# A graph layer's node loop: h and z transposed through memory in quarters instead of on TensorE, and 23 scatters moved into the pair stage

## The chip, the cores and the metric

The kernel runs on one core of one Trainium2 chip, in one launch. The metric is the device time in microseconds; several runs give a median. Besides there is one execution under the hardware profiler. Its engines are PE (TensorE), DVE (VectorE), ACT (ScalarE), POOL (GpSimd) and SP (SyncE, which only issues transfers here).

## The reference

A layer of a graph attention network with a feed-forward part, on 50,000 nodes of 256 features and 12,500 edges, in fp32. Every node also has an edge to itself.

```python
h = jnp.maximum(_layernorm(x, axis=-1), 0.0)
# _L0_gnn_ref(h): attention over edges (8 heads of 32), then
out = jax.ops.segment_sum(msg, dst, num_segments=n)
out = out.reshape(n, H * C) + bias
h = _layernorm(out + x, ln1_g, ln1_b)                # here x is the h from above
ff = jax.nn.gelu(h @ ffn_W1.T + ffn_b1, approximate=False) @ ffn_W2.T + ffn_b2
return _layernorm(h + ff, ln2_g, ln2_b)
# and at the end: x = x + _L0_gnn_ref(...)
```

Only some 12,000 nodes at most have an edge besides the one to themselves. The kernel therefore computes messages and a correction record for the destinations of the 12,500 edges, and a node loop computes for all 50,000 nodes h @ W_src (the node's edge to itself), adds its record or an empty one, and runs the feed-forward part.

## The kernel before

**Number form.** Each product of fp32 matrices is made of three matmuls on fp32r halves: an operand is split into `hi` (a rounded copy, made on ScalarE) and `lo` (the rest, `x - hi`, made on VectorE), and hi·hi, hi·lo and lo·hi are summed.

**Stages.** Setup until about 26 us: loads of indices and weights on SyncE, L442 to L465, edges brought into the order of their destination. Then the pair stage until about 315 us: 49 pairs of 128-edge chunks; GpSimd gathers the rows of x at both ends with an indirect DMA, four issues a pair (`gather`, L583), each waiting for ScalarE's relu (L385) to have freed the buffer; TensorE transposes and projects, VectorE makes the messages, SyncE stores them (`msgs`). Then softmax scans on VectorE until about 380 us; then the sum stage until about 508 us: SyncE loads the messages back (`load_pair`, 256 KB each, up to SB = 19 buffers), VectorE weighs them (L1115), TensorE sums them by destination. In that stage GpSimd runs 98 scatters (`place`, L593), each writing which record belongs to a node, and each waiting for the fourth before it. Between them stand the reciprocal deviations of the first three node groups (`input_rstd`, L599 and L601) at RSTD_AT = (8, 20, 84), for which ScalarE's `input_relu` (L728) of groups 0, 1 and 2 waits. A short fix of records that cross a chunk follows.

**Node loop.** From about 520 us to the end: 98 groups of 512 rows (4 tiles of 128, 256 features). A tile of h or z is 512 KB. Each engine has its own program of the loop, written out by hand in the function `nodes(i)` of its block; engines meet on semaphores only, and an engine takes its instructions strictly in that order. In turn i, with m counting the 8 pieces of the hidden layer of 1024:

- TensorE: `ffn1_piece` (L1342) of each m, `ffn2_piece` (L1357 to L1359) of m − 2; `turn_input` (L1367), 8 transposes of h of group i+2 into PSUM (`ps_t`) at m = 2; `turn_z` (L1389), 8 transposes of z of group i+1 at m = 4; `lift_tile` (L1379), h @ W_src, twice two tiles at m = 5 and 6.
- ScalarE: `input_relu` (L728) of group i+2, then gelu 0 (L753, L754), gelu 1, `first_norm` of i+1 (L767, makes z), gelu 2, `input_hi` (L760, copies from `ps_t`), gelus 3 and 4, `z_hi` (L775), gelus 5 to 7.
- VectorE: `act_rest` m (L1207, the lo half of gelu m), and between those `lift_add` (L1141), `first_stats` (L1147 to L1155), `add_ffn` (L1173), `input_lo` (L1160), `second_stats` (L1179 to L1186), `centre` (L1190), `z_rest` (L1165), `finish` (L1199, makes the output tile), `input_stats` (L908 to L916, of group i+3).
- GpSimd: `first_rstd` (L629, L631), `input_residual` (L641), `second_rstd` (L635), `gather_records` of i+3 (L623, four indirect DMAs), a wait for `finish`, `first_residual` (L646, L648, two operations 128x1024), `input_rstd` of i+3 (L599, L601).
- SyncE: the load of x of group i+4 (`xb`, 512 KB, L474), the store of the output of group i−1 (L517).

The node groups of x have four buffers, h two, z one.

## Time and profile before

| | us |
|---|---|
| median of 3 runs | 3205.0 |
| lowest, highest | 3204.89, 3207.64 |
| profiled execution: its own time | 3220.57 |
| its span | 3218.7 |

| engine | busy us | share of the span |
|---|---|---|
| PE | 2983.5 | 93% |
| DVE | 2242.2 | 70% |
| ACT | 1803.1 | 56% |
| POOL | 1725.5 | 54% |

Busy time is summed over instructions of an engine. A matmul's end is modelled, and matmuls overlap, so that a busy PE isn't a PE at its peak. A row of a timeline has the start in us, the duration, engine, line, operation, what it writes and reads, how many of them the row holds, and in brackets how long the engine sat idle before and which instruction's end released it. `arena` stands for all tiles that share one large buffer. The releaser is inferred from semaphores. A DMA issue's row in section 6 of the page has the median time from issue to landing.

### The profile page before, as it was taken

What the parts mean: (1) busy time and instruction counts of PE and PEld (TensorE: products, weight loads), DVE (VectorE), ACT (ScalarE), POOL (GpSimd) and SP (SyncE); (2) the same over time, 40 slices, a digit from 0 to 9 for tenths busy, and PEclk for the clock granted to TensorE, in tenths of its full rate; (3) what the DMA queues carried; (4) which work ended last, traced back from release to release, by engine and by line L of the source; (5) the groups of instructions that cost most, each with busy time, mean ns of one, the idle gap of its engine ahead of it and who ended that gap; (6) DMA issues with size and microseconds to landing.
All of it is one profiled execution on the core that took longest, in us unless ns stands there. A gap on an engine that the chain in (4) does not pass through costs nothing.

```text
span 3218.7 us, 56922 instructions
## 1 busy us (share of the span) xinstructions
PE 2983.5 (93%) x19965; PEld 2702.6 (84%) x19965; DVE 2242.2 (70%) x6228; ACT 1803.1 (56%) x3373; POOL 1725.5 (54%) x1494
## 2 busy tenths in 40 slices
PE   4887246999999999999999999999999999999998
PEld 4776235999999998999999999899999999899997
DVE  6887544777777777777777777777777777777775
ACT  4776243555555555555555555555555555555554
POOL 5765464555555555555555555555555555555552
PEclk9999577999999999999999999999999999999999
DMA  5446564222222222222222222222222222222210
GB/s 154 146 144 134 104 168 103 51 57 57 59 59 57 60 60 60 60 60 60 60 60 60 60 60 60 58 53 57 57 58 58 59 59 60 60 60 60 60 47 27
DMA packets 86976, 228.72 MB, mean 71 GB/s; under 512 B 19353, under 2 KB 23487, under 8 KB 86692
## 3 DMA queue, kind: packets, MB, share of 16 engines
q1 hardware_dynamic: 53803, 145.86, 13.7%
q0 software_dynamic: 31664, 78.07, 12.8%
q8 instruction: 161, 2.64, 0.3%
q10 hardware_dynamic: 1225, 1.15, 0.1%
q14 instruction: 123, 1.01, 0.1%
HBM read 146.85 MB, written 78.20 MB: 70 GB/s over the span
## 4 chain that ended last, share of the span: by engine, by line
PE 79%; DVE 2%; ACT 1%; issue 1%; POOL 1%; DMA 0%; DVEq 0%; POOLq 0%; ACTq 0%
PE ps_f L1342 33%; PE ps_a L1357 11%; PE ps_a L1359 11%; PE ps_a L1358 11%; PE ps_x L1379 8%; PE ps_t L1389 3%; PE ps_t L1367 2%; DVE act_lo L1207 1%; DVE arena L1147 0%; ACT h L728 0%; ACT ps_f L754 0%; DVE n_stat L908 0%; POOL n_rstd L599 0%; ACT arena L767 0%; ACT act_hi L753 0%
## 5 line engine op out<-in xcount | busy, mean ns | idle before, releaser
L1207 DVE TENSOR_TENSOR act_lo<-ps_f,act_hi 128x512 fp32r<-128x512 f32 x784 | 539.1, 688 | 732.1 <-ACT ps_f L754 731.4
L753 ACT ACTIVATE act_hi<-ps_f,hidden_bias 128x512 fp32r<-128x512 f32 x784 | 537.2, 685 | 849.1 <-PE ps_f L1342 849.1
L1357 PE MATMUL ps_a<-ffn_hi,act_hi 128*128 128x256 f32 x3136 | 892.0, 284 | 3.3 <-DVE arena L1173 3.3
L1359 PE MATMUL ps_a<-ffn_hi,act_lo 128*128 128x256 f32 x3136 | 876.6, 280 | 0.0
L1358 PE MATMUL ps_a<-ffn_lo,act_hi 128*128 128x256 f32 x3136 | 875.0, 279 | 0.0
L1342 PE MATMUL ps_f<-zt_hi,ffn_hi 128*128 128x512 f32 x1568 | 623.7, 398 | 3.3 <-DVE zt_lo L1165 1.6
L1357 PEld LDWEIGHTS ps_a<-ffn_hi,act_hi 128*128 128x128 f32 x3136 | 588.0, 187 | 41.5 <-issue 5.6
L1342 PE MATMUL ps_f<-zt_hi,ffn_lo 128*128 128x512 f32 x1568 | 619.8, 395 | 0.0
L1342 PE MATMUL ps_f<-zt_lo,ffn_hi 128*128 128x512 f32 x1568 | 619.6, 395 | 0.0
L1358 PEld LDWEIGHTS ps_a<-ffn_lo,act_hi 128*128 128x128 f32 x3136 | 589.2, 188 | 27.7
L1359 PEld LDWEIGHTS ps_a<-ffn_hi,act_lo 128*128 128x128 f32 x3136 | 588.8, 188 | 0.0
L754 ACT ACTIVATE ps_f<-ps_f,hidden_bias 128x512 f32<-128x512 f32 x784 | 509.9, 650 | 0.0
L623 POOL DMA_INDIRECT arena<-sums,node_rows x392 | 391.2, 998 | 114.4 <-issue 114.4
L629 POOL TENSOR_TENSOR arena<-arena,minus_half 128x4 f32<-128x4 f32 x98 | 98.8, 1008 | 593.5 <-DVE arena L1155 593.5
L635 POOL TENSOR_TENSOR arena<-arena,minus_half 128x4 f32<-128x4 f32 x98 | 99.8, 1019 | 497.6 <-DVE arena L1186 497.6
L1342 PEld LDWEIGHTS ps_f<-zt_hi,ffn_lo 128*128 128x128 f32 x1568 | 294.5, 188 | 73.1
L767 ACT ACTIVATE arena<-arena 128x256 f32<-128x256 f32 x392 | 203.8, 591 | 259.2 <-POOL arena L631 259.2
L1342 PEld LDWEIGHTS ps_f<-zt_hi,ffn_hi 128*128 128x128 f32 x1568 | 294.2, 188 | 42.8 <-DVE act_lo L1207 4.0
L1342 PEld LDWEIGHTS ps_f<-zt_lo,ffn_hi 128*128 128x128 f32 x1568 | 294.7, 188 | 35.2
L728 ACT ACTIVATE h<-xb,n_shift,n_rstd 128x256 f32<-128x256 f32 x392 | 203.8, 591 | 119.8 <-POOL n_shift L601 119.8
L646 POOL TENSOR_TENSOR arena<-arena,rows 128x1024 f32<-128x1024 f32 x98 | 234.8, 2396 | 17.2 <-DVE arena L1199 11.8
L648 POOL TENSOR_TENSOR arena<-arena,rows 128x1024 f32<-128x1024 f32 x98 | 235.2, 2400 | 7.7
(230 smaller groups left out, 5345.4 us busy)
## 6 DMA issues: line engine op xcount, KB each, us to landing
xb<-in_x SPq DMA_DIRECT2D x98, 512.0 KB, 6.0
out<-arena SPq DMA_DIRECT2D x98, 512.0 KB, 5.2
msgs<-arena SPq DMA_DIRECT2D x49, 256.0 KB, 2.5
arena<-msgs SPq DMA_DIRECT2D x49, 256.0 KB, 7.1
sums<-arena SPq DMA_DIRECT2D x49, 256.0 KB, 5.4
arena<-sums,node_rows POOLq DMA_INDIRECT x392, 3.8
xb<-in_x,arena POOLq DMA_INDIRECT x196, 2.8
arena<-in_w_t SPq DMA_DIRECT2D x2, 1024.0 KB, 7.5
```

Source lines behind the costliest of these rows:

```text
L623: pool.indirect_dma_start(rec[:, g.par, t, :], None, sums, bass.IndirectOffsetOnAxis(ap=at, axis=0)).then_inc(rec_in[g.par], 16)
L646: pool.tensor_tensor(res[:, n.par], z, wide(rows[:, 1:2, :], [P, TG, D]), ALU.mult).then_inc(res_part, 1)
L648: pool.tensor_tensor(res[:, n.par], res[:, n.par], wide(rows[:, 2:3, :], [P, TG, D]), ALU.add).then_inc(res_ready, 1)
L728: act.activation(h[:, a.par, t, :], xb[:, node_buf(a), t, :], ACT.Relu, bias=n_shift[:, a.par, t:t + 1], scale=n_rstd[:, a.par, t:t + 1]). ...
L753: act.activation(act_hi[:, m % AB, :], ps_f[:, m % 2, :], ACT.Gelu, bias=hidden_bias[:, m:m + 1]).then_inc(act_hi_ready, 1)
L754: act.activation(ps_f[:, m % 2, :], ps_f[:, m % 2, :], ACT.Gelu, bias=hidden_bias[:, m:m + 1]).then_inc(act_f_ready, 1)
L1207: dve.tensor_tensor(act_lo[:, m % AB, :], ps_f[:, m % 2, :], act_hi[:, m % AB, :].bitcast(F32), ALU.subtract).then_inc(act_lo_ready, 1)
L1342: ins = pe.matmul(ps_f[:, m % 2, :], ffn1[a][:, k, m * P:(m + 1) * P], zt[b][:, i.par, k, :], start=(j == 0), stop=(j == 3 * KC - 1))
L1357: pe.matmul(to, act_hi[:, m % AB, cols], ffn2[0][:, m, :], start=(m == 0 and t % 2 == 0), stop=False, skip_group_check=True)
L1358: pe.matmul(to, act_hi[:, m % AB, cols], ffn2[1][:, m, :], start=False, stop=False, skip_group_check=True)
L1359: ins = pe.matmul(to, act_lo[:, m % AB, cols], ffn2[0][:, m, :], start=False, stop=(m == MF - 1), skip_group_check=True)
L1379: ins = pe.matmul(to, xt[b][:, k, t * P:(t + 1) * P], lift[c][:, k, :], start=(j == 0 and t % 2 == 0), stop=(j == 3 * KC - 1), skip_group_ ...
```

## The change

**Transposes.** For h of groups from 2 on and z of groups from 1 on, TensorE no longer transposes. SyncE stores the 512 KB tile into DRAM (`h_rows`, `z_rows`, rows of 1 KB), waits until it has landed, and loads it back in four quarters: each fills 32 partitions, with pieces of 64 floats (256 bytes), 512 of them in a quarter. VectorE turns the blocks of 32x32 with one operation on 128x1024 (`turn`), which completes the transposition with the 256 features in another order over the partitions; the first weights (`w1`, `w_lift` and the columns `b1_col`, `g1_col`) are loaded in that order, in quarters, 12 issues more on SyncE, and `ident` is added to `w_lift` in 8 small operations instead of 2. ScalarE's copy to hi and VectorE's subtraction to lo become one operation on 1024 columns each, and read the turned tile in SBUF instead of PSUM. The first groups keep TensorE's transposes, with their columns written in the new order.

**Order in the loop.** On VectorE, `turn_input` stands before act_rest 2, `finish` before act_rest 5 instead of behind it, `turn_z` and `input_stats` before act_rest 6, and `z_rest` behind it. ScalarE's `z_hi` is at m = 5. On SyncE the two stores and eight quarter loads stand ahead of the load of x and the store of the output.

**Scatters.** 23 of the 98 are issued in the pair stage, one behind the gathers of every second pair from pair 4 to 48. RSTD_AT is moved, so that 8, 18 and 58 scatters behind the pairs stand ahead of the three `input_rstd`. SB is 18.

```diff
-SB = 19
+SB = 18
 SBN = 4
 RO = 4
 SPLITS = 9
 NB = 4
 TURN_AT = (1, 8)
-RSTD_AT = (8, 20, 84)
+PLACE_AT = range(4, 49, 2)
+RSTD_AT = (len(PLACE_AT) + 8, len(PLACE_AT) + 18, len(PLACE_AT) + 58)
...
+            def quarter(q):
+                return slice(SQ * q, SQ * q + SQ)
...
-            sp.dma_start(w1, w1_t.rearrange("(k p) n -> p k n", p=P)).then_inc(hidden_in, 16)
-            sp.dma_start(b1_col, b1_cols).then_inc(hidden_in, 16)
+            for q in range(QS):
+                sp.dma_start(w1[quarter(q)], rows_of(w1_t, q)).then_inc(hidden_in, 16)
+                sp.dma_start(b1_col[quarter(q)], cols_of(b1, q), allow_slow_non_contiguous=True).then_inc(hidden_in, 16)
-            sp.dma_start(w_lift, w_src_t.rearrange("(k p) n -> p k n", p=P)).then_inc(rows_in, 16)
-            sp.dma_start(g1_col, g1_cols).then_inc(rows_in, 16)
+            for q in range(QS):
+                sp.dma_start(w_lift[quarter(q)], rows_of(w_src_t, q)).then_inc(rows_in, 16)
+                sp.dma_start(g1_col[quarter(q)], cols_of(g1, q), allow_slow_non_contiguous=True).then_inc(rows_in, 16)
...
+            def quarters(n, tile, rows_n, stored_n, landed, turned, to):
+                wait_count(sp, landed, 64 * (n - 1))
+                sp.dma_start(rows_n[n % 2].rearrange("(t p) d -> p t d", p=P), tile).then_inc(stored_n, 16)
+                sp.wait_ge(stored_n, 16 * (n + 1))
+                wait_count(sp, turned, n)
+                for q in range(QS):
+                    sp.dma_start(to[SQ * q:SQ * q + SQ, :, :], rows_n[n % 2].rearrange("(j n) (q e) -> q n j e", n=SQ, q=QS)[q]).then_inc(landed, 16)
             def nodes(i):
-                g, o = i + 4, i - 1
+                g, o, n, a = i + 4, i - 1, i + 1, i + 2
+                if a.exists(NG):
+                    sp.wait_ge(nh_ready, TG * a.n + TG)
+                    quarters(a.n - 2, h[:, a.par, :, :], h_rows, h_stored, h_quarters, h_turned, hq)
+                if n.exists(NG):
+                    sp.wait_ge(z_ready, n.n + 1)
+                    quarters(n.n - 1, z, z_rows, z_stored, z_quarters, z_turned, zq)
...
+                if j.n == PLACE_AT[0]:
+                    pool.wait_ge(target_ready, 1)
+                    pool.wait_ge(rows_cleared, 16 * RB)
+                if j.n in PLACE_AT:
+                    place(Step(0, PLACE_AT.index(j.n), NCH))
             pool.wait_ge(in_order, 1)
             steps(pool, pair, 0, NPAIR, *PAIR_LOOP)
-            pool.wait_ge(target_ready, 1)
-            pool.wait_ge(rows_cleared, 16 * RB)
-            steps(pool, place, 0, NCH, NCH, NCH, RB)
+            steps(pool, place, len(PLACE_AT), NCH, NCH, NCH, RB)
...
-                wait_count(act, nt_turned, KC * (a.n - 1))
+                wait_count(act, nt_turned, KC * min(a.n - 1, 2))
+                wait_count(act, h_stored, 16 * (a.n - 3))
...
+                if a.n >= 2:
+                    act.wait_ge(h_turned, a.n - 1)
+                    act.copy(xt[0][:, :, :], h_t).then_inc(nt_hi, KC)
+                    return
...
+                if n.n >= 1:
+                    act.wait_ge(z_turned, n.n)
+                    act.copy(zt[0][:, n.par, :, :], z_t).then_inc(zt_hi, KC)
+                    return
...
-                    if m == 4 and norm:
+                    if m == (5 if on else 4) and norm:
...
+            def turn(n, landed, of, to, turned):
+                dve.wait_ge(landed, 64 * (n + 1))
+                dve.transpose(to.rearrange("p k n -> p (k n)"), of.rearrange("p j (k f) -> p k j f", k=KC)).then_inc(turned, 1)
+            def turn_input(a):
+                wait_count(dve, nt_lo, KC * a.n)
+                turn(a.n - 2, h_quarters, hq, h_t, h_turned)
+            def turn_z(n):
+                wait_count(dve, zt_lo, KC * n.n)
+                turn(n.n - 1, z_quarters, zq, z_t, z_turned)
...
+                    dve.tensor_tensor(xt[1][:, :, :], h_t, xt[0][:, :, :].bitcast(F32), ALU.subtract).then_inc(nt_lo, KC)
...
+                    dve.tensor_tensor(zt[1][:, n.par, :, :], z_t, zt[0][:, n.par, :, :].bitcast(F32), ALU.subtract).then_inc(zt_lo, KC)
...
+                if front and on:
+                    turn_input(a)
                 if on:
                     act_rest(i, 2)
                 if front and on:
@@ -1232,16 +1328,20 @@
                     centre(o)
                 if on:
                     act_rest(i, 4)
-                if norm:
-                    z_rest(n)
-                if on:
-                    act_rest(i, 5)
                 if back:
                     finish(o)
                 if on:
-                    act_rest(i, 6)
+                    act_rest(i, 5)
+                if norm and on:
+                    turn_z(n)
+                if norm and not on:
+                    z_rest(n)
                 if g.exists(NG) and g.n > 2:
                     input_stats(g)
+                if on:
+                    act_rest(i, 6)
+                if norm and on:
+                    z_rest(n)
                 if on:
                     act_rest(i, 7)
...
-                    if m == 4 and norm:
+                    if m == 4 and norm and not on:
                         turn_z(n, front)
-                    if m == 2 and front and on:
-                        turn_input(a)
```

VectorE in a steady turn of the node loop, before, from `act_rest` 1 on (L1207 is `act_rest`, L1173 `add_ffn`, L1160 `input_lo`, L1179 to L1186 `second_stats`, L1190 `centre`, L1165 `z_rest`, L1199 `finish`):

```order
L1207 TENSOR_TENSOR act_lo<-ps_f,act_hi 128x512
L1173 TENSOR_TENSOR arena<-ps_a,arena 128x512 x2
L1207 TENSOR_TENSOR act_lo<-ps_f,act_hi 128x512
L1160 TENSOR_TENSOR xt_lo<-ps_t,xt_hi 128x512 x2
L1179 BN_STATS arena<-arena 128x6 x4
L1183 BN_AGGR arena<-arena 128x2 x4
L1186 TENSOR_SCALAR arena<-arena 128x4
L1207 TENSOR_TENSOR act_lo<-ps_f,act_hi 128x512
L1190 SCALAR_TENSOR_TENSOR arena<-arena,rows 128x256 x4
L1207 TENSOR_TENSOR act_lo<-ps_f,act_hi 128x512
L1165 TENSOR_TENSOR zt_lo<-ps_t,zt_hi 128x512 x2
L1207 TENSOR_TENSOR act_lo<-ps_f,act_hi 128x512
```

The same engine after the change, first from `add_ffn` (now L1267) to `second_stats` (L1231 is `turn`, L1301 `act_rest`, L1246 `input_lo`):

```order
L1267 TENSOR_TENSOR arena<-ps_a,arena 128x512 x2
L1231 STREAM_TRANSPOSE arena<-arena 128x1024
L1301 TENSOR_TENSOR act_lo<-ps_f,act_hi 128x512
L1246 TENSOR_TENSOR xt_lo<-arena,xt_hi 128x1024
L1273 BN_STATS arena<-arena 128x6 x4
```

and then from `finish` (L1293) to `act_rest` 7 (L979 to L987 are `input_stats`, L1255 `z_rest`):

```order
L1293 SCALAR_TENSOR_TENSOR arena<-arena 128x256 x4
L1301 TENSOR_TENSOR act_lo<-ps_f,act_hi 128x512
L1231 STREAM_TRANSPOSE arena<-arena 128x1024
L979 BN_STATS n_stat<-xb 128x6 x4
L983 BN_AGGR n_mv<-n_stat 128x2 x4
L986 TENSOR_SCALAR n_var<-n_mv 128x4
L987 TENSOR_SCALAR n_mm<-n_mv 128x4
L1301 TENSOR_TENSOR act_lo<-ps_f,act_hi 128x512
L1255 TENSOR_TENSOR zt_lo<-arena,zt_hi 128x1024
L1301 TENSOR_TENSOR act_lo<-ps_f,act_hi 128x512
```

Two turns have come in, one ahead of `act_rest` 2 and so of `input_lo` and `second_stats`; `z_rest` has moved behind `finish`, `input_stats` and `act_rest` 6.

SyncE in a steady turn, before (a store of the output, a load of x):

```order
L517 DMA out<-arena 128x1024
L474 DMA xb<-in_x 128x1024
L517 DMA out<-arena 128x1024
L474 DMA xb<-in_x 128x1024
```

and after:

```order
L548 DMA h_rows<-h 128x4x256
L552 DMA arena<-h_rows 32x16x64 x4
L548 DMA z_rows<-arena 128x4x256
L552 DMA arena<-z_rows 32x16x64 x4
L508 DMA xb<-in_x 128x1024
L566 DMA out<-arena 128x1024
```

Ten issues now stand between one output store and the next load of x. 

GpSimd behind the pair stage's gathers, before (L593 is `place`, L599 and L601 are `input_rstd`):

```order
L593 DMA row_of<-arena 50304x1 x8
L599 TENSOR_TENSOR n_rstd<-n_var,minus_half 128x4
L601 TENSOR_TENSOR n_shift<-n_mm,n_rstd 128x4
L593 DMA row_of<-arena 50304x1 x12
L599 TENSOR_TENSOR n_rstd<-n_var,minus_half 128x4
L601 TENSOR_TENSOR n_shift<-n_mm,n_rstd 128x4
L593 DMA row_of<-arena 50304x1 x64
L599 TENSOR_TENSOR n_rstd<-n_var,minus_half 128x4
```

and after (L632 is `gather`, L642 `place`, L648 and L650 are `input_rstd`), from the last gathers on:

```order
L642 DMA row_of<-arena 50304x1
L632 DMA xb<-in_x,arena 128x256 x8
L642 DMA row_of<-arena 50304x1 x9
L648 TENSOR_TENSOR n_rstd<-n_var,minus_half 128x4
L650 TENSOR_TENSOR n_shift<-n_mm,n_rstd 128x4
L642 DMA row_of<-arena 50304x1 x10
L648 TENSOR_TENSOR n_rstd<-n_var,minus_half 128x4
L650 TENSOR_TENSOR n_shift<-n_mm,n_rstd 128x4
L642 DMA row_of<-arena 50304x1 x40
L648 TENSOR_TENSOR n_rstd<-n_var,minus_half 128x4
```

The 64 scatters between the second and the third `input_rstd` have become 40, and a scatter stands between the gathers of every other pair.

## Rows read from the trace of the kernel before

**Rows 1.** Stretch of the node loop: busy us by engine, clock, DMA share
```profile
1500.00:3000.00 1500.00, 1497.86 (x10117) 1364.12 (x10115) 1065.33 (x2910) 863.62 (x1540) 803.47 (x660) 1.00 0.22 59
```

**Rows 2.** Timeline of ScalarE and TensorE: start, duration, operation, [idle before <- releaser]
```profile
572.03 1.03 PE L1367 MATMUL ps_t<-ident,h 128*128 128x128 f32 x8
619.67 2.08 ACT L728 ACTIVATE h<-xb,n_shift,n_rstd 128x256 f32<-128x256 f32 x4 [0.54 <-POOL n_shift L601]
626.13 1.03 PE L1367 MATMUL ps_t<-ident,h 128*128 128x128 f32 x8
674.11 2.08 ACT L728 ACTIVATE h<-xb,n_shift,n_rstd 128x256 f32<-128x256 f32 x4 [0.56 <-POOL n_shift L601]
680.55 1.03 PE L1367 MATMUL ps_t<-ident,h 128*128 128x128 f32 x8
```

**Rows 3.** Timelines of GpSimd (POOL), ScalarE (ACT), VectorE (DVE): one steady group
```profile
2038.17 1.04 POOL L599 TENSOR_TENSOR n_rstd<-n_var,minus_half 128x4 f32<-128x4 f32 x1 [0.17 <-DVE n_mm L916]
2039.53 2.08 ACT L728 ACTIVATE h<-xb,n_shift,n_rstd 128x256 f32<-128x256 f32 x4 [0.56 <-POOL n_shift L601]
2042.75 0.69 DVE L1207 TENSOR_TENSOR act_lo<-ps_f,act_hi 128x512 fp32r<-128x512 f32 x1 [1.86 <-ACT ps_f L754]
2045.63 1.01 POOL L629 TENSOR_TENSOR arena<-arena,minus_half 128x4 f32<-128x4 f32 x1 [6.14 <-DVE arena L1155]
2046.95 2.08 ACT L767 ACTIVATE arena<-arena 128x256 f32<-128x256 f32 x4 [2.35 <-POOL arena L631]
2050.18 0.69 DVE L1207 TENSOR_TENSOR act_lo<-ps_f,act_hi 128x512 fp32r<-128x512 f32 x1 [2.83 <-ACT ps_f L754]
2051.98 1.39 DVE L1179 BATCH_NORM_STATS2 arena<-arena 128x6 f32<-128x256 f32 x4
2054.18 1.02 POOL L635 TENSOR_TENSOR arena<-arena,minus_half 128x4 f32<-128x4 f32 x1 [4.91 <-DVE arena L1186]
2055.38 1.03 POOL L623 DMA_INDIRECT arena<-sums,node_rows  x1 [0.18 <-issue]
...
2065.40 1.05 POOL L599 TENSOR_TENSOR n_rstd<-n_var,minus_half 128x4 f32<-128x4 f32 x1 [0.18 <-DVE n_mm L916]
```

**Rows 4.** Groups in 0 to 320 us: line, shape; busy, mean ns
```profile
L698 ACT CAST ffn_hi<-arena 128x1024 fp32r<-128x1024 f32 x2 | 2.0, 1042 | 0.0
L853 DVE TENSOR_TENSOR ffn_lo<-arena,ffn_hi 128x1024 fp32r<-128x1024 f32 x2 | 2.4, 1216 | 0.0
```

**Rows 5.** The page's DMA queues, and issues (KB, us to landing)
```profile
q1 hardware_dynamic: 53803, 145.86, 13.7%
q0 software_dynamic: 31664, 78.07, 12.8%
...
out<-arena SPq DMA_DIRECT2D x98, 512.0 KB, 5.2
msgs<-arena SPq DMA_DIRECT2D x49, 256.0 KB, 2.5
```

**Rows 6.** Timelines of the setup: SyncE's last input issue, VectorE's wait
```profile
12.63 0.43 SPq L454 DMA_DIRECT2D rows<-in_ffn_b  x1
...
26.19 0.23 DVE L889 CAST arena<-arena 98x130 f32<-98x130 int32 x1 [4.14 <-DMA arena<-line]
```

**Rows 7.** Timelines of VectorE and GpSimd in the sum stage
```profile
488.82 0.68 DVE L1115 TENSOR_TENSOR arena<-arena 128x512 f32<-128x512 f32 x1
...
492.34 2.35 POOL L641 TENSOR_TENSOR arena<-xb,rows 128x1024 f32<-128x1024 f32 x1
492.85 2.40 DVE L1115 TENSOR_TENSOR arena<-arena 128x512 f32<-128x512 f32 x1
```

**Rows 8.** GpSimd's waits in 60 to 280 us: us in total, times, longest
```profile
POOL xb L583 <- ACT h L385: 41.2, 61, 4.0
```

**Rows 9.** Timeline of ScalarE: input relus of groups 1 and 2
```profile
353.86 2.07 ACT L728 ACTIVATE h<-xb,n_shift,n_rstd 128x256 f32<-128x256 f32 x4 [32.43 <-POOL n_shift L601]
...
464.43 2.07 ACT L728 ACTIVATE h<-xb,n_shift,n_rstd 128x256 f32<-128x256 f32 x4 [29.05 <-POOL n_shift L601]
```

65 lines of the change are left out of this document (49 added, 16 removed).

## The prediction

> **What bounds the kernel now.** I read the busy time by stretch first, then the starts of two marked instructions in the first groups, then one steady group of the node loop engine by engine. The node loop (98 groups, from 520 us to the end) is most of the span, and there TensorE looks like the bound: in 1500 to 3000 us it is busy 1497.86 of 1500 us at full granted clock, VectorE 1065, ScalarE 864, GpSimd 803 [rows 1]. But a busy TensorE here is overlapped matmuls with modelled ends, so I ask who sets the pace. In the first groups TensorE's transposes of h (L1367) start at 572.03 and, two groups later, at 626.13, that is 27.05 us a group, while the relu of the input (L728) starts at 619.67 and 674.11, that is (674.11 − 619.67)/2 = 27.22 us a group, and each time on a wait for GpSimd's L601 [rows 2]. TensorE runs at 27.05 until it has caught up with the relus; two groups further its L1367 stands at 680.55, (680.55 − 626.13)/2 = 27.21 a group, as the relus. Two engines that start with different periods and end with the slower one: something other than TensorE has a period of 27.22, and TensorE's own is at most 27.05. 96 periods of 27.22 are 2613 us of the 3218.7.
>
> What has that period is a ring of waits through the other three engines. In one group [rows 3]: L601 ends and releases the relu at 2039.53; gelu 0 comes behind the relu on ScalarE, and VectorE's L1207 waits for it until 2042.75; then the statistics L1147 to L1155, on which GpSimd's L629 waits until 2045.63; on that ScalarE's first norm L767 waits until 2046.95; gelu 2 is queued behind it, and L1207 waits until 2050.18; then input_lo (L1160), second statistics from 2051.98, on which GpSimd's L635 waits until 2054.18; then on GpSimd without a pause four gathers (the first at 2055.38, 1.03 us, with 0.2 to 0.3 to the next), two residuals of 2.4 (L646 and L648), and L599 again at 2065.40, whose L601 releases the next relu. From L599's start at 2038.17 to 2065.40 it is 27.23 us. No link of this ring is a TensorE instruction. The reading order matters: the chain that ended last puts 79% of the span on TensorE, since a chain followed back stays on an engine that never visibly idles.
>
> **The node loop: what goes.** 16 transposes on TensorE for each group: twice 1.03 us per 8 [rows 2], some 0.9 each net of overlap, −1.8. TensorE's period falls to about 25.2. On the path this is worth 0, since the ring covers it: the order of GpSimd's node work and the relu's place in ScalarE's queue are the same after the change, and every other link stands too. The one link that can shorten is VectorE's input_stats, now ahead of act_rest 6: L599 waits 0.18 for it [rows 3], so −0.1.
>
> **input_lo.** It stands in the ring between 2050.18 and 2051.98. Now it is two 512-wide subtractions, of which the first starts as soon as the first half of ScalarE's copy is there. It becomes one 1024-wide copy, then one 1024-wide subtraction from SBUF. The nearest rows of those shapes are 1.04 us (L698) and 1.22 us (L853) [rows 4]. Gelu 2 ends at about 2050.1; copy until 2051.15, subtraction until 2052.3, less some 0.05 of overlap: second statistics 0.3 later than 2051.98. Term: **+0.3** (0.2 to 0.4).
>
> **The quarters of h.** VectorE's new turn of h stands ahead of act_rest 2, so in the ring: if the quarters land late, everything in it is late. The relu ends at 2041.6 (2039.53 + 2.08). SyncE stores 512 KB. A store of 256 KB took 2.5 us [rows 5]; for the other half, the hardware queue spent 13.7% × 16 engines × 3218.7 us on 145.86 MB, which is 48 ns per KB and engine, so 256 KB more are 0.8 us: landed at 2044.9. Then SyncE wakes and issues four quarters, about 0.45 apart (the issue of 0.43 in [rows 6] and a gap), the last at 2046.7; each moves 128 KB in 512 pieces of 256 bytes. The turn is 1024-wide; I cost it like L853, 1.22. To end by 2050.18 it must start by 2048.96, so the last quarter has 2.3 us from its issue, and the four have 4.1 from the landing of the store. Fixed part of a landing: 2.5 us less the 256 KB at 48 ns per KB over 16 engines (0.8) is 1.7. What a piece costs isn't in this trace; three bounds by its rows. If a quarter of a KB takes a quarter of the time (12 ns), 128 pieces per engine are 1.5 us in all, hidden behind the issues but for the last quarter's 0.4: 2046.7 + 1.7 + 0.4 = 2048.8, and the lateness x is 0. If a piece costs what 1 KB costs (48 ns), 128 pieces are 6.1 us: 2044.9 + 0.45 + 1.7 + 6.1 = 2053.2, x = 4.2. If it costs what the gathers' packets cost (12.8% × 16 × 3218.7 / 78.07 MB = 84 ns per KB) [rows 5], 128 × 84 ns are 10.8 us and x is 8.9. At 24 ns, twice the size's share, it is 3.1 us for a tile, the last landing at 2050.2, x = 1.2. I take **+0.8** (0 to 8.9), between 12 and 24 ns and nearer to 24: a packet surely has a part that doesn't shrink with it, and the out store of 512 KB took 5.2 us instead of 3.3 [rows 5], so this chain may start late too. Also in that window are the other transfers of the group (x rows, output, gathers), which share the 16 engines; the share in use is 0.22 [rows 1] and the change adds about as many packets again, so landings don't get quicker.
>
> The Trainium skill ("DMA: Bandwidth & Descriptors", section "Why small descriptors are slow") says that a 256-byte piece to or from HBM takes 11 cycles of which 8 are data, a loss of 27%, and carries 32 bytes more. By that a piece would be some 16 ns as an estimate and x would be 0: the sum would be rival 2's. No row of this trace has such pieces on this queue.
>
> **z's quarters** have the same path from first_norm's end at 2049.0 (store to 2052.3, quarters to about 2056 to 2057). The turn of z stands behind act_rest 5 (at about 2058.7), not in the ring, with over 1 us of cover; z_hi and z_rest follow by 2063 and TensorE needs them at about 2066. Cost 0; at 48 ns a piece the cover is gone, and act_rest 6 waits behind it, which is part of the dear case. The load of xb and the store of out now come behind both transfers in SyncE's queue, each of which holds it for the 3 to 4 us that a store takes to land, 14 or so of 27. Four buffers of xb cover that: 0.
>
> **Turns on VectorE.** 2 × 1.22 = 2.4 us per group. VectorE's idle time before act_rest 2 is 2.83 [rows 3], where the turn of h falls; the turn of z falls in idle time of the same kind before act_rest 6. 0 on the path, when in time.
>
> **The shared port.** input_lo and z_rest lose their PSUM input and get two SBUF inputs. At 492.85 a 128x512 operation with both inputs in SBUF (L1115) took 2.40 us, where its neighbour took 0.68, and it ended just as GpSimd's tensor operation (L641, 492.34 + 2.35) did [rows 7]. In the new order z_rest comes behind act_rest 6, at about 2062.6, right where GpSimd's second residual starts (2065.40 less 2.4 and a gap, 2062.8). If z_rest is first, GpSimd waits up to 1.2 us, in the ring. If GpSimd is first, z_rest waits until 2065.2, outside the ring, and TensorE has gained the 1.8 us that it may then wait. Bounds 0 and 1.2; I take a quarter: **+0.3**. The Trainium skill states this as a rule ("SBUF — State Buffer", section "Who interferes with whom": two SBUF inputs contend with a GpSimd instruction that reads SBUF, and the later one is blocked for all of it). The row agrees.
>
> **Loop:** −0.1 + 0.3 + 0.8 + 0.3 = +1.3 per group, so 28.5, over 96 groups: **+125** (+19 with x and lock 0; +430 at x 4.2 without the lock).
>
> **Before the loop.** Setup: SyncE has 12 more issues ahead of the row that the line's sort waits for; the 17 of now end at 12.63 + 0.43 = 13.06, at most 0.77 each, and the cheapest takes 0.43 and a gap of 0.04 [rows 6], and VectorE's L889 sits 4.14 us until that load lands. 12 × 0.47 = 5.6 to 12 × 0.77 = 9.2, taken **+7**. Pairs: 23 scatters at the 1.26 from one indirect issue to the next [rows 3] are 29 us of GpSimd, which is idle 41.2 us between gathers in 61 waits [rows 8]; some 0.3 of each wait is no slack, so 23 are cover: 6 over, less what the last pairs don't need, **+4** (0 to 10). Sum stage: ScalarE stands 32.43 us before the relu of group 1 and 29.05 before that of group 2, both for L601, which stands behind scatters [rows 9]. Before, 20 and then 64 more scatters stood ahead; now 18 and 40. The 64 took 464.43 − 353.86 = 110.6 us, 1.73 each. So the first wait gets 4 shorter, and the second relu would be at 350 + 40 × 1.73 = 419, before ScalarE reaches it at 435.4 (464.43 − 29.05): its 29 us are gone. **−4 − 29**. Against that, with 18 buffers for 19 and the load path closer behind, some comes back: **+4** (0 to 20, since the sum stage has its own loads and scatters). Together **−18** (−35 to +3).
>
> **Sum:** span 3218.7 + 125 − 18 = 3326; in the profiled execution's time 3220.6 + 107 = 3327. The median of the runs is 3205.0, 15.6 lower: **3312**. (Measurement can't tell less than about 0.2%, 6.4 us, from no change.)
>
> **Rivals.**
> 1. *Small pieces are dear.* At 48 ns a piece x is 4.2 and the lock falls away, since z_rest no longer meets the residual: 27.2 − 0.1 + 0.3 + 4.2 = 31.6 a group, +422: 3205 + 422 − 18 = 3609. At 36 ns x is 2.7 and it is 3465. For it: gathers at 84 ns per KB. Against: the store's 48 ns per KB is mostly data. Chance 0.20.
> 2. *Quarters in time, no lock.* Loop +0.2 × 96 = 19, before it −18: 3205. Decides: a piece under about 18 ns. For it: no row shows a fixed cost. Chance 0.22, with both signs round no change.
> 3. *The sum stage gives all* (faster): as 2, but the two relu stalls go and nothing comes back, −35: 3205 + 19 − 35 = 3189, down to 3180. It decides from a sum stage that shortens by its 33 us of ScalarE idle. For it: the stall is on ScalarE, which stays behind the sums. Against: what bounds the scatters is a wait on the fourth before. Chance 0.10.
> 4. *TensorE sets the pace after all:* 27.2 − 1.9 = 25.3 per group, −180: 3205 − 180 − 18 = 3007. It would need the ring to be slack, and [rows 2] speak against. Chance 0.06.
> 5. My forecast, 3230 to 3400: 0.42.
>
> **Numbers.** Range 3180 to 3500: it holds 5, 2, 3 and half of 1, 0.84. Faster: 4, 3 and a small part of 2, 0.20. Same: 0.10. Slower: 0.70.
>
> **What the changed profile would show.** Relu starts 28.5 apart, with L601's wait before each; 27.4 for rival 2, 31 for 1, 25.3 for 4. Idle time of VectorE before the turn of h ended by a DMA: 2 to 3 us of it mean x near 0 or below, more means late. TensorE idle some 3 us a group. z_rest or the second residual at over 1.5 or 3 us shows the lock. Relu of group 2 near 440 with no wait. I am wrong if the ring can move: if GpSimd's gathers or residuals start earlier against the relu than now.

## The result and the profile after

The changed kernel takes 3310.3 us (median of 4 runs, 3307.1 to 3314.5) against 3204.9 before: a ratio of 1.0329, 95% interval 1.0311 to 1.0346. It is slower, by 105 us. Its profiled execution took 3314.5 us, its span 3312.8, 94.1 more than the span of before.

Two numbers are worked out from the start times in the traces, here and for all kernels below, over the relus between 700 and 3000 us: the **period** of the node loop is the mean distance from one input relu to the next, and an **offset** is the mean distance from a relu to a later instruction of the same turn.

| | before | after |
|---|---|---|
| period | 27.30 | 28.77 |
| relu of group 3, the first in the loop | 565.07 | 519.03 |
| relu of group 97, the last | 3130.94 | 3224.10 |
| offset of second statistics | 12.45 | 13.18 |
| offset of input_rstd on GpSimd | 25.94 | 26.42 |
| duration of input_rstd's first operation | 1.05 | 2.04 |

From the relu of group 3 to that of group 97 the loop grew by 2705.1 − 2565.9 = 139 us; up to group 3 the kernel gained 46 us; the sum, 93, is the difference of the spans but for one. The two traces are not of the same standing: that of before is of an execution 15.6 us above the median it is compared with, that of after of one 4.3 us above. So the split of 139 and −46 is that of the traces' 94 us, and the 105 us between the medians leave 11 that it does not place.

The stretch of the node loop that answers to [rows 1], with the transfer queue that answers to [rows 5] and the page's issues:

```profile
1500.00:3000.00 1500.00, 1359.61 (x8759) 1208.60 (x8758) 1214.78 (x2768) 818.75 (x1356) 810.59 (x624) 1.00 0.48 129
```

```profile
q1 hardware_dynamic: 563771, 348.29, 36.1%
...
out<-arena SPq DMA_DIRECT2D x98, 512.0 KB, 3.4
z_rows<-arena SPq DMA_DIRECT2D x97, 512.0 KB, 2.9
arena<-z_rows SPq DMA_DIRECT2D x388, 128.0 KB, 2.8
h_rows<-h SPq DMA_DIRECT2D x96, 512.0 KB, 2.9
arena<-h_rows SPq DMA_DIRECT2D x384, 128.0 KB, 2.8
```

TensorE is no longer busy all the time (1360 of 1500 us, against the 1498 of [rows 1]), VectorE went from 1065 to 1215. A store of 512 KB lands 2.9 us after its issue, and a quarter in 2.8.

One group of the new loop, which answers to [rows 3]; first VectorE and GpSimd around z_rest (L1255), the second residual (L705) and input_rstd (L648), with ScalarE's relu (L787) behind it:

```profile
2068.61 2.94 DVE L1255 TENSOR_TENSOR zt_lo<-arena,zt_hi 128x1024 fp32r<-128x1024 f32 x1
...
2068.07 2.40 POOL L705 TENSOR_TENSOR arena<-arena,rows 128x1024 f32<-128x1024 f32 x1
2070.43 2.03 POOL L648 TENSOR_TENSOR n_rstd<-n_var,minus_half 128x4 f32<-128x4 f32 x1
...
2072.77 2.08 ACT L787 ACTIVATE h<-xb,n_shift,n_rstd 128x256 f32<-128x256 f32 x4 [1.23 <-POOL n_shift L650]
```

z_rest starts 0.5 us behind the residual, stands until that has ended at 2070.47, and then does its work of 1.1 us; GpSimd's next operation, which took 1.05 us in [rows 3], starts at 2070.43 and ends 0.9 us after z_rest, at 2072.46. So the two block each other one after the other, and the second block is in the ring (the loop of waits through GpSimd, ScalarE and VectorE that the prediction found): the relu waits for it. In all 82 groups between 700 and 3050 us z_rest starts behind the residual. Then the turn (L1231), input_lo (L1246) and second statistics (L1273) of the same group, and SyncE's transfers for them:

```profile
2074.88 0.37 SPq L548 DMA_DIRECT2D h_rows<-h  x1
2077.81 1.91 SPq L552 DMA_DIRECT2D arena<-h_rows  x4
```

```profile
2082.00 1.25 DVE L1231 STREAM_TRANSPOSE arena<-arena 128x1024 f32<-128x1024 f32 x1 [1.42 <-DMA arena<-h_rows]
2083.41 0.69 DVE L1301 TENSOR_TENSOR act_lo<-ps_f,act_hi 128x512 fp32r<-128x512 f32 x1 [0.17 <-ACT ps_f L813]
2084.51 1.23 DVE L1246 TENSOR_TENSOR xt_lo<-arena,xt_hi 128x1024 fp32r<-128x1024 f32 x1 [0.40 <-ACT xt_hi L819]
2085.65 1.40 DVE L1273 BATCH_NORM_STATS2 arena<-arena 128x6 f32<-128x256 f32 x4
```

Here the quarters are in time for act_rest 2 (L1301), which waits for the gelu, 0.17 us, and not only for the turn. Second statistics start 12.88 us behind the relu, the smallest offset of all groups is 12.84, and the mean 13.18. Most groups are later than this one, only a little of it through act_rest 2, whose mean offset is 10.77 against 10.65 before. ScalarE's copy to hi (L819) also waits for the turn, and input_lo waits for the copy. The copy starts at 10.89 on average against 10.56 before, and in 75 of 80 groups later than 10.60. What ScalarE waits for from 1500 to 3000 us, in us in total, times, and the longest:

```profile
ACT h L787 <- POOL n_shift L650: 73.4, 52, 2.9
ACT xt_hi L819 <- DVE arena L1231: 11.2, 31, 1.0
```

The first row is the ring's link: the relu waits for GpSimd in each of the 52 groups.

### The profile page after: what moved, and what is told of

Same layout as the page of the kernel before. It is cut to its first block, busy times and chain, and to the rows that moved or that the text cites. A ratio compares the mean times of both kernels' runs of the same rounds, so it can differ in the third digit from the quotient of the medians.

```text
span 3312.8 us, 55297 instructions
## 1 busy us (share of the span) xinstructions
PE 2868.0 (87%) x18421; PEld 2545.1 (77%) x18421; DVE 2615.5 (79%) x6234; ACT 1803.1 (54%) x3180; POOL 1818.3 (55%) x1497
## 4 chain that ended last, share of the span: by engine, by line
POOL 43%; issue 24%; DVE 8%; ACT 7%; PE 2%; DMA 1%; POOLq 0%; SPq 0%; DVEq 0%; ACTq 0%
POOL arena L675 11%; POOL arena L703 7%; POOL arena L705 7%; POOL arena L693 7%; POOL n_rstd L648 6%; DVE arena L1218 4%; ACT h L787 3%; POOL arena L681 3%; POOL arena L687 3%; DVE act_lo L1301 2%; ACT act_hi L812 2%; ACT ps_f L813 2%; PE ps_f L1442 1%; DVE arena L1222 1%; POOL n_shift L650 1%
## 5 line engine op out<-in xcount | busy, mean ns | idle before, releaser
L1442 PE MATMUL ps_f<-zt_hi,ffn_hi 128*128 128x512 f32 x1568 | 642.5, 410 | 144.3 <-DVE act_lo L1301 127.6
L1301 DVE TENSOR_TENSOR act_lo<-ps_f,act_hi 128x512 fp32r<-128x512 f32 x784 | 537.4, 685 | 277.8 <-ACT ps_f L813 274.3
L1231 DVE STREAM_TRANSPOSE arena<-arena 128x1024 f32<-128x1024 f32 x193 | 239.7, 1242 | 165.3 <-DMA arena<-h_rows 161.8
L1255 DVE TENSOR_TENSOR zt_lo<-arena,zt_hi 128x1024 fp32r<-128x1024 f32 x97 | 279.1, 2878 | 0.0
L787 ACT ACTIVATE h<-xb,n_shift,n_rstd 128x256 f32<-128x256 f32 x392 | 203.8, 591 | 138.4 <-POOL n_shift L650 138.4
```

The costliest lines, as they stand in the source:

```text
L787: act.activation(by_half(to) if a.n < 2 else to, by_quarter(of) if a.n < 2 else of, ACT.Relu, bias=n_shift[:, a.par, t:t + 1], scale=n_rst ...
L1231: dve.transpose(to.rearrange("p k n -> p (k n)"), of.rearrange("p j (k f) -> p k j f", k=KC)).then_inc(turned, 1)
L1255: dve.tensor_tensor(zt[1][:, n.par, :, :], z_t, zt[0][:, n.par, :, :].bitcast(F32), ALU.subtract).then_inc(zt_lo, KC)
L1301: dve.tensor_tensor(act_lo[:, m % AB, :], ps_f[:, m % 2, :], act_hi[:, m % AB, :].bitcast(F32), ALU.subtract).then_inc(act_lo_ready, 1)
L1442: ins = pe.matmul(ps_f[:, m % 2, :], ffn1[a][:, k, m * P:(m + 1) * P], zt[b][:, i.par, k, :], start=(j == 0), stop=(j == 3 * KC - 1))
```

## The experiments

All are compared by the ratio to the kernel before on the same chip. Chips differ: before took 3205 us beside the changed kernel, 3219 beside e1 to e4, 3217 beside e5 to e8, 3220 beside e9 and e10, and 3274 beside e11 and e12. The period of before is from its one trace.

| kernel | period | ratio to before, 95% interval |
|---|---|---|
| before | 27.30 | 1 |
| changed | 28.77 | 1.0329, 1.0311 to 1.0346 |
| e1_scatters | 27.31 | 0.9856, 0.9839 to 0.9872 |
| e2_h_quarters | 28.14 | 1.0116, 1.0099 to 1.0133 |
| e3_z_quarters | 27.96 | 1.0048, 1.0031 to 1.0064 |
| e4_psum | 27.75 | 1.0007, 0.9996 to 1.0019 |
| e5_cut_before | 27.05 | 0.9919, 0.9903 to 0.9936 |
| e6_cut_after | 27.78 | 1.0013, 1.0004 to 1.0023 |
| e7_cut_scatters_before | 27.05 | 0.9771, 0.9755 to 0.9788 |
| e8_cut_psum_after | 27.73 | 1.0006, 0.9996 to 1.0015 |
| e9_early_cut_psum | 27.42 | 0.9898, 0.9881 to 0.9915 |
| e10_early_cut | 27.45 | 0.9901, 0.9885 to 0.9918 |
| e11_rest3_early_cut_psum | 25.77 | 0.9652, 0.9616 to 0.9688 |
| e12_rest3_early_cut | 28.00 | 1.0268, 1.0244 to 1.0291 |

### The parts of the change, one at a time

**e1_scatters**: the kernel before with the scatters alone.

```diff
-RSTD_AT = (8, 20, 84)
+PLACE_AT = range(4, 49, 2)
+RSTD_AT = (len(PLACE_AT) + 8, len(PLACE_AT) + 18, len(PLACE_AT) + 58)
...
                 gather(j)
...
+                if j.n in PLACE_AT:
+                    place(Step(0, PLACE_AT.index(j.n), NCH))
...
-            steps(pool, place, 0, NCH, NCH, NCH, RB)
+            steps(pool, place, len(PLACE_AT), NCH, NCH, NCH, RB)
```

> The kernel before with the 23 scatters in the pair stage and the new places of the three input_rstd, nothing else; the node loop is untouched, 27.3 us a group. In the changed kernel the first relu of the loop (group 3) started at 519.0 against 565.1, 46 us earlier, although its setup had 12 more issues (last load of the setup 5.6 us later). Theory (the scatters alone carry this gain, and the setup's issues took some back): about 3205 - 46 - 5 = 3154 us. Rival (the prediction's term of -4 - 29 + 4 + 4 for scatters is right, the rest came from elsewhere in the change): about 3180 us.

Measured: 3173.0 against 3219.1, 46 us less, with the loop unchanged at 27.31; the relu of group 3 starts at 515.67. The scatters are worth all of the gain ahead of the loop.

**e2_h_quarters** and **e3_z_quarters**: the changed kernel with one of the two tiles back on TensorE. First e2, z back (w1, b1_col and g1_col are loaded as before, z_rest and z_hi stand where they stood):

```diff
-                    quarters(n.n - 1, z, z_rows, z_stored, z_quarters, z_turned, zq)
...
-                if norm and on:
-                    turn_z(n)
...
-                    if m == 4 and norm and not on:
+                    if m == 4 and norm:
                         turn_z(n, front)
```

> The changed kernel with only h through memory; z is transposed on TensorE again, z_rest reads PSUM and stands before act_rest 5, finish behind it. Theory (of the 1.47 us by which a group grew, 1.0 is the shared port between z_rest and GpSimd, 0.7 input_lo and late quarters, -0.2 input_stats): a group takes 27.3 + 0.7 = 28.0, so 3310 - 0.8 * 96 = about 3235 us; L648 back from 2.04 to 1.05 us. Rival (the growth is all h's: quarters and the turn in the ring): 28.8 a group, 3305 us.

Then e3, h back (w_lift is loaded as before):

```diff
-                    quarters(a.n - 2, h[:, a.par, :, :], h_rows, h_stored, h_quarters, h_turned, hq)
...
-                if front and on:
-                    turn_input(a)
...
+                    if m == 2 and front and on:
+                        turn_input(a)
```

> The changed kernel with only z through memory; h is transposed on TensorE again. Theory (as above): second statistics are back at 12.45 us behind the relu, z_rest still takes 2.9 us and L648 2.0 us; a group takes 27.3 + 1.0 - 0.2 = 28.1, about 3310 - 0.7 * 96 = 3243 us. Rival (the growth is all h's): 27.1 a group, 3150 us.

Measured: e2 28.14 us a group, +34 us in all; e3 27.96, +16 us. The growths of 0.84 and 0.66 us a group sit where the theory has them. From 1500 to 3000 us, e2's z_rest and input_rstd, then e3's:

```profile
L1242 DVE TENSOR_TENSOR zt_lo<-ps_t,zt_hi 128x512 fp32r<-128x512 f32 x106 | 67.7, 680 | 0.0
...
L644 POOL TENSOR_TENSOR n_rstd<-n_var,minus_half 128x4 f32<-128x4 f32 x53 | 55.4, 1046 | 0.0
```

```profile
L1241 DVE TENSOR_TENSOR zt_lo<-arena,zt_hi 128x1024 fp32r<-128x1024 f32 x53 | 155.6, 2936 | 0.0
...
L645 POOL TENSOR_TENSOR n_rstd<-n_var,minus_half 128x4 f32<-128x4 f32 x53 | 107.8, 2034 | 0.0
```

In e2 GpSimd's operation is back at 1.05 us, but second statistics are at an offset of 13.50; in e3 it takes 2.03, and second statistics are back at 12.45. Both rivals, that all of it was h's, fall. The two growths add up to 1.50, about the 1.47 of the change, but this is in part by chance: e2's quarters of h come later than those of the changed kernel (the turn at an offset of 9.85 against 9.53), so that its second statistics are 1.05 later than before instead of 0.73, and both runs have the gain between second statistics and input_rstd. Why e2's quarters are later stays unexplained. e3 was expected 38 us above the 3205 of before and is 16 above its own; 13 of the difference are its 0.14 us a group, and the rest is open.

**e4_psum**: the turns write the PSUM tile.

```diff
-        h_t, z_t = part([KC, GR]), part([KC, GR])
...
+        h_t = z_t = ps_t[:, :, :]
```

> The changed kernel, whose two turns write their result to PSUM (the tile of the transposes of before) instead of SBUF; so input_lo and z_rest have one input in SBUF again. All else as changed. Theory (z_rest is blocked by GpSimd's residual L705, and then blocks L648, because both of its inputs are in SBUF): z_rest about 1.3 us instead of 2.9, L648 1.05 instead of 2.04, a group 28.77 - 1.0 = 27.8, 3310 - 96 = about 3215 us. Rival (z_rest and L648 are long for another reason, such as GpSimd's own load or the transfers): no change, 3310 us.

Measured: 27.75 us a group, and a ratio of 1.0007 to before, 3.1% under the change; as expected. Its z_rest and the two operations of GpSimd:

```profile
2041.84 1.21 DVE L1255 TENSOR_TENSOR zt_lo<-ps_t,zt_hi 128x1024 fp32r<-128x1024 f32 x1
...
2041.30 2.41 POOL L705 TENSOR_TENSOR arena<-arena,rows 128x1024 f32<-128x1024 f32 x1
2043.67 1.05 POOL L648 TENSOR_TENSOR n_rstd<-n_var,minus_half 128x4 f32<-128x4 f32 x1
```

z_rest lies at the same place beside the residual, does as much work, and neither is held up. The only thing that changed for it is where one of its inputs lies. So the lock is 28.77 − 27.75 = 1.02 us a group, 98 of the 139 us by which the loop grew. That the whole comes out at the time of before is a coincidence: the loop is still 48 us longer than in before (2613.5 us from the relu of group 3 to that of group 97, against 2565.9), and the scatters take 48 off ahead of it.

### Is it a ring, or TensorE?

**e5_cut_before**, **e6_cut_after**, **e7_cut_scatters_before**, **e8_cut_psum_after**: the same edit in four kernels: before, the changed one, e1 and e4. GpSimd's input_rstd goes ahead of the gathers, and VectorE's input_stats up into its idle time behind add_ffn.

```diff
                 if o.exists(NG):
                     second_rstd(o)
+                if g.exists(NG) and g.n > 2:
+                    input_rstd(g)
                 if g.exists(NG):
                     gather_records(g)
...
                     first_residual(n)
-                if g.exists(NG) and g.n > 2:
-                    input_rstd(g)
...
                 if back:
                     add_ffn(o)
+                if g.exists(NG) and g.n > 2:
+                    input_stats(g)
...
-                if g.exists(NG) and g.n > 2:
-                    input_stats(g)
```

> The kernel before with the ring of waits cut and nothing else changed: VectorE's input_stats moved from between act_rest 6 and 7 up behind add_ffn (into its idle 2.8 us), GpSimd's input_rstd moved ahead of the four gathers, so that neither gathers nor residuals stand between second_rstd and the next relu. Theory (a ring through GpSimd, ScalarE and VectorE sets 27.30 us a group and TensorE alone would need at most 27.05): 27.05 a group or a little less, -24 us, 0.75% less than before, and relus that start without a wait for GpSimd. Rival (TensorE set the pace all along): no change.

> The kernel before with the 23 scatters in the pair stage and the cut of the ring, transposes on TensorE. The two should add: 27.05 a group and 46 us off the part before the loop, 3205 - 46 - 24 = 3135 us. If TensorE set the pace all along: as e1_scatters, 3159 us.

Measured: e5 27.05 us a group and 0.81% less (0.75% expected); e7 2.29% less, the sum of e1 and e5. No TensorE instruction was touched, and the loop is faster; its stretch and two of its relus:

```profile
1500.00:3000.00 1500.00, 1500.00 (x10203) 1373.09 (x10202) 1047.60 (x2935) 866.89 (x1552) 822.20 (x665) 1.00 0.22 60
```

```profile
1503.97 2.07 ACT L728 ACTIVATE h<-xb,n_shift,n_rstd 128x256 f32<-128x256 f32 x4
1530.99 2.07 ACT L728 ACTIVATE h<-xb,n_shift,n_rstd 128x256 f32<-128x256 f32 x4
```

The brackets with the wait for L601 are gone, and the period varies by 0.06 us only: now TensorE sets it, at the 27.05 that the first groups of before had shown. e7, with the transposes on TensorE, beats both kernels.

> The changed kernel with the same cut of the ring. Theory (the change had taken 1.9 us a group off TensorE, which the ring hid): a group falls from 28.77 to about 26 us (TensorE alone: 25.2; the shared port may hold VectorE up), 3310 - 2.8 * 96 = about 3045 us. Rival 1 (TensorE or its rhythm with ScalarE and VectorE bounds this kernel too): 28.8 a group, 3310 us. Rival 2 (another wait closes right behind, VectorE with its turns and the blocked z_rest): 27.2 to 27.8 a group, 3160 to 3215 us.

> The changed kernel with the cut of the ring and with the two turns written to PSUM. Theory (the shared port costs only where VectorE or GpSimd is waited for; once the ring is cut, TensorE waits for zt_lo at most): up to 0.5 us a group less than e6_cut_after, which would be 3000 to 3045 us. Rival (the port's 1.6 us in z_rest is then on VectorE's path, which is the bound): 1.0 to 1.6 a group less than e6_cut_after.

Measured: 27.78 and 27.73, not the 26 that I expected: the second rival of e6. The ring is cut (the relus wait for nothing), and another wait closes 1 us behind it. e8's shorter z_rest (1.21 against 2.30 us) is worth only 0.05 us a group there. And the cut is worth nothing over e4, which has 27.75 with the ring whole: without the lock the ring is no longer than what stands behind it. Where e6's TensorE waits, 1500 to 3000 us:

```profile
PE ps_f L1442 <- DVE act_lo L1301: 87.3, 64, 1.8
```

That is 1.6 us a group, and 27.8 − 1.6 is 26.2: about what TensorE needs without the transposes.

### The ring behind the ring

**e9_early_cut_psum** (and **e10_early_cut**, with the turns in SBUF): on top of that cut, ScalarE's relu goes from ahead of gelu 0 to behind gelu 5 of the turn before.

```diff
-                    if m == 0 and front and a.n > 2:
-                        input_relu(a)
...
+                    if m == 5 and g.exists(NG) and g.n > 2:
+                        input_relu(g)
```

> e8_cut_psum_after with ScalarE's input_relu moved from ahead of gelu 0 to behind gelu 5 of the turn before (ScalarE stands idle there), nothing else. In e6_cut_after TensorE waits 1.6 us a group for act_lo, and the relu starts with no wait behind gelu 7: theory: a second ring has taken the place of the cut one, from gelu 7 over the relu (2.0 us), gelu 0, first statistics, first_norm, gelu 2 and the turn of h to act_rest 2, and from there TensorE's pieces 4 to 7 back to gelu 7. With the relu out of it a group takes what TensorE needs, 25.3 to 26 us: 27.7 less 1.7 to 2.4, so 165 to 230 us less than e8_cut_psum_after, about 3000 to 3050 us. Rival (VectorE's load with the turns, or ScalarE's, is the bound): no gain over 0.5 us a group, 3170 us or more.

> As e9_early_cut_psum, but the turns write SBUF, so that input_lo and z_rest have two SBUF inputs, as in the changed kernel. If the shared port costs only where someone waits for VectorE or GpSimd there: TensorE needs zt_lo at the next group's start, z_rest is blocked for 1 to 1.7 us, and e10 takes 0 to 0.7 us a group more than e9, 0 to 70 us. If VectorE is the bound: 1 us or more a group, 100 us or more.

Measured: 27.42 and 27.45, 0.3 us a group less than e8, and not 1.7 to 2.4. The theory fell, and its rival's bound of 0.5 us held: the relu was not what the new ring hung on. VectorE no longer waits for the quarters of h at all, and TensorE still waits 1.5 us a group. e9's waits of TensorE, 1500 to 3000 us:

```profile
PE ps_f L1442 <- DVE act_lo L1301: 80.7, 57, 1.8
```

In one turn of e9, TensorE stands from 2019.03 to 2020.47 ahead of piece 5, and act_rest 3, for which it waits, ends at 2020.41: it is queued behind turn, act_rest 2, input_lo and the whole of second_stats (L1273 to L1280).

```profile
2014.07 1.25 DVE L1231 STREAM_TRANSPOSE ps_t<-arena 128x1024 f32<-128x1024 f32 x1
2015.23 0.67 DVE L1301 TENSOR_TENSOR act_lo<-ps_f,act_hi 128x512 fp32r<-128x512 f32 x1
2016.55 1.23 DVE L1246 TENSOR_TENSOR xt_lo<-ps_t,xt_hi 128x1024 fp32r<-128x1024 f32 x1 [0.65 <-ACT xt_hi L819]
2017.69 1.40 DVE L1273 BATCH_NORM_STATS2 arena<-arena 128x6 f32<-128x256 f32 x4
...
2019.72 0.69 DVE L1301 TENSOR_TENSOR act_lo<-ps_f,act_hi 128x512 fp32r<-128x512 f32 x1
2020.47 0.50 PE L1442 MATMUL ps_f<-zt_hi,ffn_hi 128*128 128x512 f32 x1 [1.44 <-DVE act_lo L1301]
```

**e11_rest3_early_cut_psum** (and **e12_rest3_early_cut**, with the turns in SBUF): act_rest 3 ahead of second_stats.

```diff
-                if back:
-                    second_stats(o)
                 if on:
                     act_rest(i, 3)
                 if back:
+                    second_stats(o)
                     centre(o)
```

> e9_early_cut_psum with VectorE's act_rest 3 moved ahead of second_stats (2.2 us), nothing else. In e9 a group takes 27.4 us, and TensorE stands still once a group for 1.5 us, ahead of piece 5, for act_lo of piece 3, which is queued on VectorE behind turn, act_rest 2, input_lo and second_stats. Theory (this is the ring that has taken the place of the cut one, TensorE's own work is 27.4 - 1.5 = 25.9): about 26.0 a group, 3187 - 135 = about 3050 us. Rival (ScalarE's first_norm and gelu 2 set it anyway, the next wait is late by about as much): 27.0 a group or more, 3150 us or more.

> The same with the turns written to SBUF as in the changed kernel. If VectorE isn't waited for at z_rest, as e9 and e10 showed (same time): as e11, within 20 us. If, at a shorter group, z_rest's blocked 1.1 us and the residual's 0.9 us meet a waiting engine: 0.3 to 1 us a group more than e11, 30 to 100 us.

Measured: e11 25.77 us a group, 1.65 less than e9, and 3.5% less than before: the fastest of all (the expected 3050 us is a time of another chip; here before took 3274 and e11 3157, and the loop is what was expected). The stretch of e11, and its waits of TensorE:

```profile
1500.00:3000.00 1500.00, 1499.07 (x9778) 1347.94 (x9777) 1228.62 (x3087) 919.14 (x1516) 880.93 (x697) 1.00 0.61 144
```

```profile
PE ps_f L1441 <- DVE act_lo L1301: 0.4, 2, 0.2
PE ps_f L1441 <- DVE zt_lo L1255: 0.2, 1, 0.2
```

TensorE is busy again, 58 groups in the stretch where before has 55. Whether e11 needs the relu's new place, or even the cut, no run shows: act_rest 3 was not moved without them. And e12, the same with both inputs of z_rest in SBUF, takes 28.00: 2.2 us a group more, 6% of the time, past both bounds that I had given it. From 1500 to 3000 us:

```profile
PE ps_f L1441 <- DVE zt_lo L1255: 94.0, 52, 2.1
...
L1255 DVE TENSOR_TENSOR zt_lo<-arena,zt_hi 128x1024 fp32r<-128x1024 f32 x54 | 165.6, 3066 | 0.0
```

A longer z_rest cost 0.03 us a group in e10 (2.31 against e9's 1.22 us). Here it takes 3.07 against e11's 1.21, and TensorE waits for zt_lo in nearly every group, since it now comes before z_rest is done.

If before's period is 27.30 on that chip too, the loop accounts for (27.30 − 25.77) × 94 = 144 us of e11's gain, which is 117 in all. Then some 27 us were lost outside the loop, where e1 won 46 on another chip. No trace of before and no run of the scatters alone was made there, so this is not shown. What the traces show is that e11's pair stage is slower (from 26 to 640 us GpSimd waits 120.4 us for ScalarE's relu L405 in e11, and 32.7 in e9) and that its relu of group 3 starts at 632.92, against 514.46 in e9. What the scatters are worth there stays open, and the steps of the period from e9 to e11 and from e10 to e12 are between chips; that from e11 to e12 is not.

## Why the prediction was right, and where not

The forecast was 3312, the time is 3310, and the reading behind it held: the loop was paced by a ring without TensorE in it, so less work on TensorE bought nothing (e5 shows the ring, e11 what the shorter TensorE is worth once nothing else is slower), and what the new steps add to the ring came on top. But the agreement to 2 us is luck. Three terms of the loop were off and nearly cancelled, −18 ahead of the loop was −46, and by the traces the change is 94 us where the sum had 107; the 11 us between the traces and the medians, which no term stands for, brought the forecast back to the measured time.

| term, us a group | predicted | measured |
|---|---|---|
| TensorE (on the path) | 0 | 0 |
| input_lo | +0.3 | +0.4 (least offset of second statistics, 12.84 − 12.45) |
| late quarters | +0.8 (0 to 8.9) | +0.34 (mean less least offset, 13.18 − 12.84) |
| input_stats earlier | −0.1 | −0.25 (0.48 of input_rstd's offset less 0.73) |
| shared port | +0.3 (0 to 1.2) | +0.99 (input_rstd 2.04 less 1.05; e4: 1.02) |
| sum | +1.3, period 28.5 | +1.47, period 28.77 |
| loop | +125 | +139 |
| ahead of the loop | −18 | −46 |

**TensorE.** The −1.8 was too large, which cost nothing since it wasn't on the path: TensorE's own period is 27.05 in e5 and 25.77 in e11, 1.3 less, both with TensorE busy all the time and at a granted clock of 1.00, though on two chips.

**The quarters.** Mis-sized by a factor of two. In the trace's record of transfers between 700 and 3050 us a piece of 256 bytes took 18.3 ns (334,445 of them) and one of 1 KB 46.4 ns. I had taken a value between 12 and 24, nearer to 24; 18.3 is the middle, and the store landed after 2.9 us instead of 3.3. But I had the deadline wrong too: I asked when the turn must end for act_rest 2 (start by an offset of 9.43), and missed that ScalarE's copy waits for it and is the tighter one (9.19). The mean turn starts at 9.53. That makes act_rest 2 only 0.12 late on average; the rest of the 0.34 comes through the copy. The Trainium skill's figure ("DMA: Bandwidth & Descriptors", section "Why small descriptors are slow"), from which I had worked out an estimate of some 16 ns and no lateness, was about as far off as my value on the other side: 11 cycles for 8 of data are 1.4 times the share of the size, and the trace has 1.6 times it against the piece of 1 KB.

**The shared port.** This was the step at which I chose worst. The place was right (z_rest beside the second residual) and so was the price of 1.2 us at its upper bound, but I took a quarter of it. I had seen two outcomes, z_rest first or GpSimd first, and held the second for free. In the trace GpSimd is first in every group, z_rest is held up for 1.7 us, and then, released, holds up GpSimd's next small operation in its turn, and that one is in the ring. A lock must be followed on both sides: who is behind the one that got the port, too. The Trainium skill's rule ("SBUF — State Buffer", section "Who interferes with whom") covers both sides: "Issue order, not op shape, decides who blocks." The traces agree: GpSimd's residual blocks z_rest in the changed kernel, and z_rest lengthens the residual in e6 (3.25 us). So does e4, z_rest 2.94 to 1.21 us and input_rstd 2.04 to 1.05 by moving one input of z_rest to PSUM.

**Ahead of the loop.** Setup was +5.6 (the last load of the setup is issued at 28.11 instead of 22.53; +7 predicted), and the relu of group 0 came at 332.87 instead of 319.36, 13.5 later, where I had +11. The mis-sized term is the sum stage: from the relu of group 0 to that of group 3 it took 186.2 us instead of 245.7, −59.5 where I had −29 (e1, the scatters alone, has 188.4). The two stalls of [rows 9] after the change, the second one without a wait:

```profile
342.64 2.07 ACT L787 ACTIVATE h<-xb,n_shift,n_rstd 128x256 f32<-128x256 f32 x4 [7.70 <-POOL n_shift L650]
...
421.84 2.06 ACT L787 ACTIVATE h<-xb,n_shift,n_rstd 128x256 f32<-128x256 f32 x4
```

The second went as predicted, −29. The first fell by 24.7, from 32.43 to 7.70, and I had −4: two scatters less at 1.73 us. But the 12 scatters between the first two input_rstd had not taken 1.73 each, they had taken (352.49 − 314.23)/12 = 3.2, since each waits for the landing of the fourth before, and these landings were slow while SyncE issued the 19 loads of the messages (316.25 to 336.31):

```profile
323.29 0.96 POOL L593 DMA_INDIRECT row_of<-arena  x1 [6.14 <-DMA row_of<-arena]
...
337.81 0.96 POOL L593 DMA_INDIRECT row_of<-arena  x1 [4.00 <-DMA row_of<-arena]
344.34 0.96 POOL L593 DMA_INDIRECT row_of<-arena  x1 [5.57 <-DMA row_of<-arena]
```

(These are rows of before.) After the change the 10 that are left start at 324.81, 4 us before those loads (329.05), and take (341.27 − 322.94)/10 = 1.8. I had taken the mean of a long undisturbed stretch for a short disturbed one. That the loads are the disturbance is read from the overlap; no run moved them alone. The remaining 6 us lie between the relus of groups 1 and 2 (2.3) and of 2 and 3 (3.5), and their cause is open. And the +4 that was to come back did not.

**Rivals.** TensorE as the pace (3007 us) is refuted by the time itself and by e5. Dear pieces (3609 us) are refuted by the 18.3 ns. "In time and no lock" (3205 us) has its second half in e4, and e4 does take the time of before, but not by that rival's sum: its quarters are late as well (second statistics at 13.25), its loop is 48 us longer where the rival had 19, and the part ahead of the loop is 48 shorter where it had 18. The third rival had the direction of the sum stage right, which gave even more than it said; the lock and the late quarters outweighed it.

## What to carry to other kernels

An engine that is busy 99.9% by the profile need not be the bound: compare its period where it runs freely with that of the waits around it, and before taking work off it, cut the ring with a reordering, which here was a few lines and 0.8% (e5). Once the cut was made, taking the transposes off TensorE paid (25.8 against 27.05 us a group), but only after two more reorderings, of which the one that gave most (1.65 us a group) was found from the one wait that TensorE's row still showed. When a step is to complete in time, look for everyone who waits for it: here a copy on ScalarE needed the turn before VectorE's next operation did. When an operation moves from PSUM to SBUF inputs, look at what GpSimd does at that time, and at what GpSimd has to do next: the same instruction cost 0, 1.0 or 2.2 us a group, depending on who was waiting (e10 against e9, the change against e4, e12 against e11).

## What the runs showed of the hardware that I had not expected

- A VectorE operation with two SBUF inputs and GpSimd's tensor operations hold each other up in both directions: z_rest took 1.21 us with one input in PSUM (e4) and 2.94 behind a residual, a 128x4 power on GpSimd 1.05 us in e4 and 2.04 behind z_rest; in e6 and e10 the residual itself took 3.25 us instead of 2.4.
- VectorE's turn of 128x1024 in blocks of 32x32 takes 1.24 us into SBUF and 1.25 us into PSUM (e4). So the way over PSUM cost nothing here, and it ended the lock.
- A store of 512 KB into DRAM, in rows of 1 KB, let SyncE go on after 2.93 us in most groups of the changed kernel (2.92 to 4.70, and under 3.1 in nine of ten), though the transfers' share of use had gone from 0.22 to 0.48. It is no constant: in e11, at a share of 0.61 and on another chip, the store of h took 4.76 us in the median.
